# Attention products in two halves of 64 rows, low parts of the exponentials on GpSimd, and four smaller moves

## Chip, core and metric

The kernel runs on one core of one Trainium2 chip. The metric is the device time of one launch over all 8 images, in microseconds (us). Before the change it is 9249.9 us, the median of 3 runs (9244.49 to 9249.97).

## What is computed

The reference has two layers on x of shape (8, 192, 64, 64). The first (`_L0_conv_ref`) is a layer norm over channels, a projection, a 3x3 depthwise convolution, a selective scan in four directions, a norm, a gate and an output projection. The second is attention over all 4096 positions of an image, with 96 channels:

```python
theta_x = _conv1x1(x, theta_w, theta_b).reshape(B, O, N)   # O = 96, N = 4096
phi_x = _conv1x1(x, phi_w, phi_b).reshape(B, O, N)
g_x = _conv1x1(x, g_w, g_b).reshape(B, O, N)
f1 = jnp.einsum('bon,bom->bnm', theta_x, phi_x)
f_div_C = jax.nn.softmax(f1, axis=-1)
y = jnp.einsum('bnm,bom->bon', f_div_C, g_x)
W_y = _conv1x1(y.reshape(B, O, H, W), W_w, W_b)
return W_y + x
```

All of the change lies in the second layer and in the step that makes its operands.

## The kernel before

Each image runs through a projection stage, a scan stage, a mix stage (`run_mix`: it finishes layer 0 chunk by chunk and makes phi, g and the first theta) and an attention stage (`run_attend`). A chunk is 512 positions (T); there are 8 chunks (NCH). Engines run in order and meet at semaphores only; the order of the work is written out by hand.

**Precision.** An operand of the attention's products is a pair of 4-byte values rounded to fp32r: the high part is the value rounded, the low part is the rest. Scores are phi high times theta high, plus phi low times theta high, plus phi high times theta low; the weighing is g high times p high, plus g low times p high, plus g high times p low, where p is the exponential. `phh`, `phl` hold phi (97 rows by 4096), `thc[par]` holds theta of a chunk twice (high and low, 97 rows by 512), `gth`, `gtl` hold g with a column of ones for the denominator.

**The shift.** The exponentials need the top score of each query subtracted. Row 96 of `phh` is 1 and row 96 of `thc[par][0]` holds minus the top, so that the scores' product adds it. For the next chunk the tops come from 32 products per chunk, high times high (`top`, L601, 96 rows), which VectorE reduces (L1384); `TOPS` (L287) says how many of them go into each step: none in step 0, 2 in steps 1 to 4, 3 in steps 5 to 12, none in 13 to 15. VectorE then reduces the 32 tops to one (`negate`, L1395) and SP writes the row with 4 DMAs (L382), which it issues behind the two stores of the chunk before (`store`, L361).

**A step.** A chunk has 16 steps (mp). Step mp on TensorE, in `attend` (L736): `scores` (L675, 6 products of 97 rows for two blocks of 128 keys, into two PSUM banks), then up to two tops, then `weigh` of step mp-2 (L698, 6 products of 128 rows, all adding into bank 4), then a third top if there is one. The other engines: ScalarE takes the exponential out of PSUM (L1014, `pf`) and rounds it (L1020, `ph`; waits until `weigh` of mp-2 has read the old one); VectorE subtracts (L1400, `pl`), after the step's tops; TensorE weighs it two steps later. In step 0 TensorE makes theta of the next chunk (L598, L599, with fp32 operands), which ScalarE copies twice (L962, L965) and VectorE subtracts (L1315, one instruction). At step 2 ScalarE reads the sum of the chunk before (L1002, `yraw`); its denominator goes to DRAM and back (`invert`, `divide`), and the output products (L732, 96 rows by 128 and by 64 columns, fp32) stand at the ends of steps 10 and 12. The last chunk has no tops and no theta; the first has nothing of a chunk before.

```python
for e in range(2):                       # scores, L687 on
    mm(dst, kk, hi[:, :], ...)           # L692
    q = mm(dst, phl[...], hi[:, :], ...) # L693
    q = mm(dst, kk, lo[:, :], ...)       # L695
```

GpSimd does nothing in the attention stage.

Of the kernel before, what the change touches and what calls it, by code (L numbers as in the profile page):

```python
# [19 lines left out]
F32 = mybir.dt.float32  # L20
# [34 lines left out]
def build(nc, nb, x, vec, w_in, w_x, w_dt, sel, fold, ident, w_out, w_att, gb, w_w, out):  # L55
# [3 lines left out]
    with ctx:  # L59
# [23 lines left out]
        rdb = sb("rdb", [O, T], where=aty)  # L83
# [7 lines left out]
        phh = sb("phh", [O + 1, L], F32R, where=kx)  # L91
        phl = sb("phl", [O + 1, L], F32R, where=kx)
# [46 lines left out]
        thc = [[sb(f"thc{q}{i}", [O + 1, T], F32R, where=vx) for i in range(2)] for q in range(2)]  # L139
# [13 lines left out]
        oa = sb("oa", [P, T], where=lnx)  # L153
        phf = sb("phf", [O, T], where=lnx)
        zs = sb("zs", [P, 2, T], where=lnx)
        cs = sb("cs", [P, 2, T], where=lnx)
        tapw = sb("tapw", [P, 6, P], where=lnx)
# [29 lines left out]
        def barrier(eng, b, n):  # L187
# [8 lines left out]
            "pads_set", "rows_zero", "row_one", "xb_zero", "bias_row", "consts_set", "dsum_set", "borders_set", "scan_set", "att_set", "thc_set", "mx_link",  # L196
# [14 lines left out]
            "thc_ready", "st_ready", "pf_ready", "ph_ready", "pl_ready", "pv_ready", "yraw_ready", "den_ready", "inv_link", "rden_ready",  # L211
# [75 lines left out]
        TOPS = [0] + [2] * 4 + [3] * 8 + [0] * 3  # L287
# [3 lines left out]
        DEN_AT, RB_AT, WY_AT, WR_AT = 5, 8, 10, 12  # L291
# [3 lines left out]
        def _(sp):  # L295
# [15 lines left out]
            with sp.Fori(0, nb) as b:  # L311
# [55 lines left out]
                def attend(c, par, before, nxt):  # L367
# [3 lines left out]
                    if before:  # L371
# [5 lines left out]
                        sp.dma_start(rdb[:, :], rden.unsqueeze(0).to_broadcast([O, T])).then_inc(S["rb_loaded"], 16)  # L377
                        store(c - 1)
                    if nxt:
                        sp.wait_ge(S["nmx_ready"], i + 2)  # L380
                        for t in range(4):
                            sp.dma_start(thc[1 - par][0][O:O + 1, t * P:(t + 1) * P].bitcast(F32), nmr[:, t:t + 1].bitcast(F32))\  # L382
                                .then_inc(S["shift_loaded"], 16)
# [8 lines left out]
        def _(pe):  # L392
# [24 lines left out]
            with pe.Fori(0, nb) as b:  # L417
# [183 lines left out]
                def top(j, i, par, t, m, bank):  # L601

                    if j == 0:
                        pe.wait_ge(S["thh_ready"], i + 1)
                    pe.wait_ge(S["top_read"], i * NU + (j + 1))
                    mm(ps[:, bank, :], thc[par][0][0:O, t * P:(t + 1) * P], phh[0:O, bass.ds(m * T, T)],  # L606
                       start=True, stop=True).then_inc(S["top_ready"], 1)

                def early_top(c, t):
# [6 lines left out]
                    mm(ps[:, 6 + t % 2, :], thc[0][0][0:O, t * P:(t + 1) * P], phh[0:O, bass.ds(m * T, T)],  # L616
# [58 lines left out]
                def scores(mp, c, i, par, first):  # L675
                    s = i * MP + mp
                    hi, lo = thc[par]
                    early = mp == 0 and first
                    if mp == 0 and not first:
                        pe.wait_ge(S["thl_ready"], i + 1)  # L680
                        pe.wait_ge(S["shift_loaded"], b * (64 * (NCH - 1)) + (c * 64 + 64))
                    pe.wait_ge(S["pf_ready"], s + 1)
                    if early:
                        for e in range(2):
                            mm(ps[:, e, :], phh[:, e * P:(e + 1) * P], lo[:, :], start=True, stop=False)
                        shift(i)
                        pe.wait_ge(S["thc_ready"], b + 1)  # L687
                    for e in range(2):
                        m = 2 * mp + e
                        dst = ps[:, 2 * (mp % 2) + e, :]  # L690
                        kk = phh[:, m * P:(m + 1) * P]
                        mm(dst, kk, hi[:, :], start=not early, stop=False)  # L692
                        q = mm(dst, phl[:, m * P:(m + 1) * P], hi[:, :], start=False, stop=early)  # L693
                        if not early:
                            q = mm(dst, kk, lo[:, :], start=False, stop=True)  # L695
                    q.then_inc(S["st_ready"], 1)

                def weigh(mp, i):  # L698
                    s = i * MP + mp
                    pe.wait_ge(S["pl_ready"], s + 3)  # L700
                    if mp == 0:
                        pe.wait_ge(S["yraw_ready"], i + 1)
                    for e in range(2):
                        m = 2 * mp + e
                        dst = ps[0:O + 1, 4, :]
                        mm(dst, gth[:, m, :], ph[:, mp % 2, e, :], start=(m == 0), stop=False)  # L706
                        mm(dst, gtl[:, m, :], ph[:, mp % 2, e, :], start=False, stop=False)  # L707
                        q = mm(dst, gth[:, m, :], pl[:, mp % 2, e, :], start=False, stop=(m == MT - 1))  # L708
                    q.then_inc(S["pv_ready"], 1)
# [26 lines left out]
                def attend(c, par, before, nxt):  # L736
                    i = i_0 + c
                    for mp in range(MP):
                        scores(mp, c, i, par, not before)
                        if mp == 0 and nxt:  # L740
                            theta(c + 1, i + 1, before)
                        blocks = range(FIRST_TOP[mp], FIRST_TOP[mp] + TOPS[mp]) if nxt else ()
                        for j in blocks[:2]:
                            top(j, i + 1, 1 - par, j // (NU // 4), j % (NU // 4), 5 + j % 2)
# [783 lines left out]
```

## Time and profile before

| what | value |
|---|---|
| median of 3 runs | 9249.9 us |
| profiled execution | 9256.15 us |
| its span | 9254.4 us |
| instructions | 103902 |
| PE busy | 8642.6 us, 93% |
| PE weight loads | 4648.4 us, 50% |
| DVE busy | 7377.0 us, 80% |
| ACT busy | 6091.9 us, 66% |
| POOL busy | 3295.4 us, 36% |

PE is TensorE, PEld its weight loads (they run beside the products), DVE VectorE, ACT ScalarE, POOL GpSimd, SP the engine that issues the DMAs. A product's time in the trace runs from its start to its last result, and products overlap, so that PE's busy share says little; the distance between the starts of two products is its pace. Lines (L692) are those of the kernel before.

### The profile page before, as it was taken

To read this page: it belongs to the slowest core of one execution; us is meant where nothing else is said; L and a number is where in the kernel's file an instruction comes from. 1 tells how busy PE (TensorE), PEld (TensorE's weight loads), DVE (VectorE), ACT (ScalarE), POOL (GpSimd) and SP (SyncE) were. 2 spreads that over 40 slices of the span, in tenths; PEclk is the share of its full clock that TensorE was granted. 3 is DMA by queue.
4 is the path that set the end of the run, shared out by engine and by line. 5 is a ranking of instruction groups with operands and counts; after the bars stand their busy time and mean duration, and the time that the engine had idled before them with its cause. 6 is when DMAs were issued, how large, how long until landed. Compare 5 with 4: busy or idle time off the path is not lost. (4 is left out here: it accounts for less than half of the span.)

```text
span 9254.4 us, 103902 instructions
## 1 busy us (share of the span) xinstructions
PE 8642.6 (93%) x26448; PEld 4648.4 (50%) x26448; DVE 7377.0 (80%) x8229; ACT 6091.9 (66%) x7440; POOL 3295.4 (36%) x1853
## 2 busy tenths in 40 slices
PE   7899998999989998899988999889998899988999
PEld 3336743367433674336733367333673336733476
DVE  6987779877798777987679876798767987689876
ACT  6765677656776567765677556775567755677566
POOL 2870028600286002860038600385003850038400
PEclk9999999999999999999999999999999999999999
DMA  1320013200132001320013200232002320023200
GB/s 53 111 87 13 10 56 112 80 13 10 57 111 82 11 11 59 115 76 10 11 63 111 76 10 11 65 116 71 8 12 68 111 73 8 11 72 114 66 8 12
DMA packets 286693, 503.21 MB, mean 54 GB/s; under 512 B 142155, under 2 KB 143215, under 8 KB 253431
## 3 DMA queue, kind: packets, MB, share of 16 engines
q1 hardware_dynamic: 286199, 497.81, 17.9%
q8 instruction: 166, 2.72, 0.1%
q14 instruction: 328, 2.69, 0.1%
HBM read 467.99 MB, written 29.47 MB: 54 GB/s over the span
## 5 line engine op out<-in xcount | busy, mean ns | idle before, releaser
L1400 DVE TENSOR_TENSOR pl<-pf,ph 128x1024 fp32r<-128x1024 f32 x1024 | 1254.3, 1225 | 1007.1 <-ACT ph L1020 999.5
L1253 DVE TENSOR_TENSOR_SCAN h<-ps,h,dbu 128x512 f32<-128x512 f32 x1536 | 1884.2, 1267 | 59.8 <-POOL dbu L1087 29.9
L1087 POOL TENSOR_TENSOR dbu<-bs,du 128x1024 f32<-128x1024 f32 x768 | 1808.1, 2369 | 54.1 <-POOL du L1078 54.1
L1020 ACT ACTIVATE ph<-pf 128x1024 fp32r<-128x1024 f32 x1024 | 1085.3, 1060 | 750.3 <-PE ps L708 750.0
L885 ACT ACTIVATE ps<-dt,negA 128x512 f32<-128x512 f32 x1536 | 1037.5, 687 | 684.8 <-DVE h L1253 684.8
L1014 ACT ACTIVATE pf<-ps 128x1024 f32<-128x1024 f32 x1024 | 1050.4, 1026 | 530.7 <-PE ps L695 513.3
L1066 POOL MEMSET pad<- 128x66 f32 (+1 forms) x64 | 7.2, 200 | 3853.2 <-DVE fa L1429 3853.0
L1384 DVE TENSOR_REDUCE mx<-ps 128x1 f32<-128x512 f32 x1792 | 1168.6, 683 | 78.8 <-PE ps L606 62.5
L1261 DVE TENSOR_TENSOR hc<-h,ps 128x1024 f32<-128x1024 f32 x768 | 937.9, 1221 | 110.3 <-PE ps L487 19.7
L487 PE MATMUL ps<-xhl,selr 128*128 128x512 f32 x1536 | 768.1, 585 | 238.8 <-DVE hc L1261 238.6
L1072 POOL TENSOR_TENSOR dt<-dt,ze 128x1024 f32<-128x1024 f32 x256 | 604.0, 2359 | 1061.3 <-ACT dt L878 1061.3
L692 PE MATMUL ps<-thc,phh 97*128 97x512 f32 x2048 | 847.2, 414 | 6.1 <-ACT thc L997 6.1
L1078 POOL TENSOR_TENSOR du<-dt,u 128x512 f32<-128x512 f32 x512 | 712.1, 1411 | 317.1 <-DVE dt L1243 316.4
L706 PE MATMUL ps<-ph,gth 128*97 128x512 f32 x2048 | 818.9, 400 | 3.2 <-ACT yraw L1002 3.2
L693 PE MATMUL ps<-thc,phl 97*128 97x512 f32 x2048 | 815.6, 398 | 0.0
L708 PE MATMUL ps<-pl,gth 128*97 128x512 f32 x2048 | 808.2, 395 | 0.0
L707 PE MATMUL ps<-ph,gtl 128*97 128x512 f32 x2048 | 807.8, 394 | 0.0
L695 PE MATMUL ps<-thc,phh 97*128 97x512 f32 x2032 | 802.2, 395 | 0.0
L487 PEld LDWEIGHTS ps<-xhl,selr 128*128 128x128 f32 x1536 | 248.1, 193 | 896.7 <-DVE hc L1261 716.5
L606 PE MATMUL ps<-phh,thc 96*128 96x512 f32 x1792 | 614.6, 403 | 18.6 <-DVE mx L1384 17.9
L528 PE MATMUL ps<-hc,eye 128*128 128x512 f32 x1024 | 484.0, 595 | 0.0
L692 PEld LDWEIGHTS ps<-thc,phh 97*128 97x128 f32 x2048 | 389.7, 190 | 171.9 <-issue 66.7
(204 smaller groups left out, 14540.6 us busy)
## 6 DMA issues: line engine op xcount, KB each, us to landing
bs<-rows SPq DMA_DIRECT2D x256, 1024.0 KB, 5.1
bs<-rows SPq DMA_DIRECT2D x512, 256.0 KB, 6.1
xa<-in_x SPq DMA_DIRECT2D x130, 256.0 KB, 2.9
xb<-in_x SPq DMA_DIRECT2D x130, 128.0 KB, 3.0
out<-fa SPq DMA_DIRECT2D x64, 256.0 KB, 2.1
rdb<-rden SPq DMA_DIRECT2D x56, 192.0 KB, 3.4
out<-fa SPq DMA_DIRECT2D x64, 128.0 KB, 2.4
xhl<-ct SPq DMA_DIRECT2D x256, 8.0 KB
```

Source lines behind the costliest of these rows:

```text
L487: m = mm(flat(ps[:, 4 + e, :]), selr[:, j * P:(j + 1) * P], src, start=True, stop=True)
L692: mm(dst, kk, hi[:, :], start=not early, stop=False)
L693: q = mm(dst, phl[:, m * P:(m + 1) * P], hi[:, :], start=False, stop=early)
L706: mm(dst, gth[:, m, :], ph[:, mp % 2, e, :], start=(m == 0), stop=False)
L885: A(ps[:, 2 + e, :], dt[par][:, 0 if j < NS else 1, :], ACT.Exp, scale=negA[:, k * NT + j:k * NT + j + 1]).then_inc(S["dA_ready"], 1)
L1014: A(pf[:, mp % 2, :, :], ps[:, 2 * (mp % 2):2 * (mp % 2) + 2, :], ACT.Exp)\
L1020: A(ph[:, mp % 2, :, :], pf[:, mp % 2, :, :], ACT.Copy).then_inc(S["ph_ready"], 1)
L1087: pool.tensor_tensor(dbu[:, q, :, :], bs[par][:, q, :, :], du[:, r:r + 1, :].to_broadcast([P, 2, T]), ALU.mult).then_inc(S["dbu_ready"], 1)
L1253: dve.tensor_tensor_scan(h[:, j, ::step], ps[:, 2 + e, ::step], dbu[:, q, e, ::step], h[:, j, end:end + 1], ALU.mult, ALU.add)\
L1261: TT(hc[:, q, :, :], h[:, 2 * q:2 * q + 2, :], ps[:, 4:6, :], ALU.mult).then_inc(S["hc_ready"], 1)
L1384: dve.tensor_reduce(mx[:, t, m:m + 1], ps[:, 5 + j % 2, :], AX.X, ALU.max)\
L1400: TT(pl[:, mp % 2, :, :], pf[:, mp % 2, :, :], ph[:, mp % 2, :, :].bitcast(F32), ALU.subtract)\
```

## The change

- **Halves of 64 rows.** phi's three tensors become `ph1` (rows 0 to 95 high, 96 to 127 high of rows 64 to 95 again), `ph2` (rows 0 to 95 low, 96 to 127 high of rows 32 to 63) and `ph3` (33 rows at partition 0 for even blocks, 33 rows at 64 for odd ones, the last of each being 1 for the shift). Theta is laid out to match in `th1`, `thx` and `thy`. Scores of a block are now five products of 64 rows or fewer, and those of two blocks are ten: six in `scores_1`, four in `scores_2`. Even products run over partitions 0 to 63 into one bank, odd ones over 64 to 127 into the other; `scores_2` turns the banks round. `weigh` becomes twelve halves, the lower rows into bank 4 and the upper into bank 5, and is split in two calls of six. A top becomes two halves into the same bank, the second waiting until the first is complete (`top_half`).
- **Order on TensorE.** A step is `scores_1` (with a third top around it), half of `weigh` (with a top), `scores_2`, the other half of `weigh` (with a top).
- **GpSimd** subtracts `pl` in the steps that have tops; VectorE in the others, one step later in its order, ahead of the tops.
- **TOPS** is now 0, 0, 2, then 3 in steps 3 to 12, 0 in 13 to 15. The output products move to the ends of steps 13 and 15.
- **The sums** of banks 4 and 5 are read by ScalarE and VectorE and added on VectorE; ScalarE reads ahead of its rounding in step 1.
- **The shift's row** is written by two DMAs of 512 elements (into `thx` and `thy`) ahead of the chunk's stores.
- ScalarE copies theta a third time (`thx`), and phi four times more in the mix stage; VectorE subtracts theta in four instructions instead of one (steps 1, 4, 5, 6).

```diff
-        TOPS = [0] + [2] * 4 + [3] * 8 + [0] * 3
+        TOPS = [0] * 2 + [2] + [3] * 10 + [0] * 3
-        DEN_AT, RB_AT, WY_AT, WR_AT = 5, 8, 10, 12
+        DEN_AT, RB_AT, WY_AT, WR_AT = 5, 8, 13, 15
+        LOW, UP = slice(0, R), slice(R, P)
+        BY_POOL = [mp for mp in range(MP) if TOPS[mp]]
...
@@ sync, attend
-                        sp.dma_start(rdb[:, :], rden...).then_inc(S["rb_loaded"], 16)
-                        store(c - 1)
+                        sp.dma_start(rdb[0:O, :], rden...).then_inc(S["rb_loaded"], 16)
                     if nxt:
                         sp.wait_ge(S["nmx_ready"], i + 2)
-                        for t in range(4):
-                            sp.dma_start(thc[1 - par][0][O:O + 1, t * P:(t + 1) * P]..., nmr[:, t:t + 1]...)
+                        for row in (thx[1 - par][LO:LO + 1, :], thy[1 - par][O:O + 1, :]):
+                            sp.dma_start(row..., nmr[:, :]...).then_inc(S["shift_loaded"], 16)
+                    if before:
+                        store(c - 1)
@@ tensor
+                def top(j, i, c, par, rows):
+                    n = b * (NU * (NCH - 1)) + c * NU + (j + 1)
+                    t, m = j // (NU // 4), j % (NU // 4)
+                    if rows == LOW:
+                        if j == 0:
+                            pe.wait_ge(S["thh_ready"], i + 1)
+                            pe.wait_ge(S["thl_ready"], i * 4 + 1)
+                        pe.wait_ge(S["top_read"], i * NU + (j + 1))
+                    else:
+                        pe.wait_ge(S["top_half"], n)
+                    q = mm(ps[:, 6 + j % 2, :], th1[par][rows, :]..., ph1[rows, m * T:(m + 1) * T],
+                           start=(rows == LOW), stop=(rows == UP))
+                    q.then_inc(S["top_half" if rows == LOW else "top_ready"], 1)
+                def scores_1(mp, c, i, par, first, j=None):
...
+                    def low(n):
+                        if n < 2:
+                            return mm(ps[:, bank, :], (ph1, ph2)[n][LOW, one], t1[LOW, :], start=(n == 0), stop=False)
+                        return scores_0(mp, par, 0)
+                    def up(n):
+                        if n < 2:
+                            return mm(ps[:, bank + 1, :], (ph1, ph2)[n][UP, other], (t1, tx)[n][UP, :], start=(n == 0), stop=False)
+                        return scores_0(mp, par, 1)
+                    if j is not None:
+                        top(j, i + 1, c, 1 - par, LOW)
+                    for n in range(2 if mp == 0 and first else 3):
...
+                    q.then_inc(S["s1_done"], 1)
+                    if j is not None:
+                        top(j, i + 1, c, 1 - par, UP)
+                def scores_2(mp, i, par, first):
+                    pe.wait_ge(S["s1_done"], i * MP + (mp + 1))
...
+                    mm(ps[:, bank, :], ph1[UP, one], t1[UP, :], start=False, stop=False)
+                    mm(ps[:, bank + 1, :], ph1[LOW, other], t1[LOW, :], start=False, stop=False)
+                    mm(ps[:, bank, :], ph2[UP, one], tx[UP, :], start=False, stop=not early)
+                    q = mm(ps[:, bank + 1, :], ph2[LOW, other], t1[LOW, :], start=False, stop=not early)
...
+                def weigh(mp, e, i, c, par=0, j=None):
...
+                    for n in range(3):
+                        if j is not None and n == 1 - e:
+                            top(j, i + 1, c, 1 - par, LOW)
+                        if j is None or n < 1 - e:
+                            half(n, 4, LOW)
+                            q = half(n, 5, UP)
+                        else:
+                            half(n, 5, UP)
+                            q = half(n, 4, LOW)
...
+                    if j is not None:
+                        top(j, i + 1, c, 1 - par, UP)
@@ scalar
+                    A(thx[par][R:O, :], thf[R:O, :], ACT.Copy).then_inc(S["thx_ready"], 1)
...
+                        A(ph1[O:P, bass.ds(c * T, T)], phf[R:O, :], ACT.Copy)
+                        A(ph2[O:P, bass.ds(c * T, T)], phf[LO:R, :], ACT.Copy)
+                        for e in range(2):
+                            A(ph3[e * R:e * R + LO, ...], blocks[:, :, e, :], ACT.Copy).then_inc(S["ph3_ready"], 1)
...
-                        if mp == LAG and before:
-                            read_sum(i - 1)
                         act.wait_ge(S["st_ready"], s + 1)
-                        act.wait_ge(S["pl_ready"], s + 1)
+                        wait_low(act, i, mp - 2)
                         A(pf[...], ps[...], ACT.Exp).then_inc(S["pf_ready"], 1)
                         if mp == 0 and nxt:
                             split_theta(i + 1, 1 - par)
+                        if mp == LAG - 1 and before:
+                            read_sum(i - 1)
@@ gpsimd
+                    for mp in BY_POOL:
+                        pool.wait_ge(S["ph_ready"], i * MP + (mp + 1))
+                        pool.tensor_tensor(pl[:, mp % 2, :, :], pf[...], ph[...], ALU.subtract).then_inc(S["plp_ready"], 1)
@@ vector
+                def read_sum(i):
+                    dve.wait_ge(S["pv_ready"], i * MP + (MP + 2))
+                    dve.tensor_copy(rdb[:, :], ps[0:O + 1, 5, :]).then_inc(S["sum5_read"], 1)
+                    dve.wait_ge(S["sum4_read"], i + 2)
+                    dve.wait_ge(S["sum5_read"], i + 2)
+                    TT(yraw[:, :], yraw[:, :], rdb[:, :], ALU.add).then_inc(S["yraw_ready"], 1)
...
-                        if mp == 1 and nxt:
-                            low_theta(i + 1, 1 - par)
+                        if mp in (1, 4, 5, 6) and nxt:
+                            low_theta(i + 1, 1 - par, (1, 4, 5, 6).index(mp))
+                        if mp == LAG and before:
+                            read_sum(i - 1)
...
+                        if mp > 0 and mp - 1 in BY_DVE:
+                            low_exp(mp - 1, i * MP + (mp - 1))
+                        for j in tops[0:]:
+                            top(j, i + 1)
```

## Rows read from the trace of the kernel before

**Rows 1.** Busy time by stretch: the attention stage of the first image.
```profile
core 0: us, PE busy (x) PEld busy (x) DVE busy (x) ACT busy (x) POOL busy (x), PEclk, DMA share, GB/s
741.00:1180.00 439.00, 435.11 (x1776) 311.13 (x1775) 309.45 (x392) 272.16 (x272) 0.00 (x0) 0.99 0.04 9
```

**Rows 2.** Timeline in the attention stage: start us, us, engine, line, operation.
```profile
849.95 0.39 PE L695 MATMUL ps<-thc,phh 97*128 97x512 f32 x1
...
850.65 0.40 PE L695 MATMUL ps<-thc,phh 97*128 97x512 f32 x1
...
851.08 1.02 ACT L1014 ACTIVATE pf<-ps 128x1024 f32<-128x1024 f32 x1 [1.71 <-PE ps L695]
...
852.27 0.39 PE L692 MATMUL ps<-thc,phh 97*128 97x512 f32 x1
```

**Rows 3.** Timeline of ScalarE: theta's first copy in two chunks that follow each other.
```profile
861.31 0.68 ACT L962 ACTIVATE thf<-ps,vecs 96x512 f32<-96x512 f32 x1 [0.86 <-PE ps L599]
...
918.11 0.68 ACT L962 ACTIVATE thf<-ps,vecs 96x512 f32<-96x512 f32 x1 [0.86 <-PE ps L599]
```

**Rows 4.** Timeline of TensorE: the first output product, later theta's two fp32 products.
```profile
840.45 1.03 PE L732 MATMUL ps<-yn,ww 96*128 96x512 f32 x2
840.91 0.79 PE L692 MATMUL ps<-thc,phh 97*128 97x512 f32 x1
841.54 0.39 PE L693 MATMUL ps<-thc,phl 97*128 97x512 f32 x1
...
859.22 1.02 PE L598 MATMUL ps<-pad,wa 128*96 x2
860.17 1.10 PE L599 MATMUL ps<-pad,wa 64*96 x2
861.20 0.47 PE L706 MATMUL ps<-ph,gth 128*97 128x512 f32 x1
861.50 0.39 PE L707 MATMUL ps<-ph,gtl 128*97 128x512 f32 x1
```

**Rows 5.** Timeline in the mix stage: products of only 96 columns, two to a line.
```profile
657.87 0.39 PE L654 MATMUL ps<-wa,na 128*128 128x96 f32 x2
658.09 0.39 PE L655 MATMUL ps<-wa,nb 128*128 128x96 f32 x2
```

**Rows 6.** Costliest groups of the page: busy us, mean ns of one, idle before.
```profile
L1400 DVE TENSOR_TENSOR pl<-pf,ph 128x1024 fp32r<-128x1024 f32 x1024 | 1254.3, 1225 | 1007.1 <-ACT ph L1020 999.5
L1087 POOL TENSOR_TENSOR dbu<-bs,du 128x1024 f32<-128x1024 f32 x768 | 1808.1, 2369 | 54.1 <-POOL du L1078 54.1
L1020 ACT ACTIVATE ph<-pf 128x1024 fp32r<-128x1024 f32 x1024 | 1085.3, 1060 | 750.3 <-PE ps L708 750.0
L1014 ACT ACTIVATE pf<-ps 128x1024 f32<-128x1024 f32 x1024 | 1050.4, 1026 | 530.7 <-PE ps L695 513.3
L1384 DVE TENSOR_REDUCE mx<-ps 128x1 f32<-128x512 f32 x1792 | 1168.6, 683 | 78.8 <-PE ps L606 62.5
```

**Rows 7.** Timeline of ScalarE in steps 0 to 2 of the second chunk.
```profile
804.52 0.68 ACT L962 ACTIVATE thf<-ps,vecs 96x512 f32<-96x512 f32 x1 [0.86 <-PE ps L599]
805.24 0.63 ACT L965 ACTIVATE thc<-thf 96x512 fp32r<-96x512 f32 x1
...
810.33 0.58 ACT L1002 ACTIVATE yraw<-ps 97x512 f32<-97x512 f32 x1
```

**Rows 8.** Timeline in the projection stage: GpSimd beside a VectorE instruction with two SBUF inputs.
```profile
169.22 0.75 DVE L1190 SCALAR_TENSOR_TENSOR u<-pad,vecs,u 128x512 f32<-128x512 f32 x1
...
170.52 2.46 POOL L1072 TENSOR_TENSOR dt<-dt,ze 128x1024 f32<-128x1024 f32 x1 [117.50 <-ACT dt L878]
...
170.79 2.73 DVE L1190 SCALAR_TENSOR_TENSOR u<-pad,vecs,u 128x512 f32<-128x512 f32 x1
```

**Rows 9.** Timeline of ScalarE in a step of the mix stage.
```profile
681.74 0.49 ACT L985 ACTIVATE gth<-ps 128x384 f32 x1 [0.34 <-PE ps L655]
...
686.26 0.63 ACT L791 ACTIVATE sqa<-da 128x512 f32<-128x512 f32 x1 [4.03 <-DVE db L1163]
```

More of the change, by code:

```diff
@@ L138, in build @@
         thf = sb("thf", [O, T], where=vx)
-        thc = [[sb(f"thc{q}{i}", [O + 1, T], F32R, where=vx) for i in range(2)] for q in range(2)]
+        th1 = [sb(f"th1{q}", [P, T], F32R, where=vx) for q in range(2)]
+        thx = [sb(f"thx{q}", [P, T], F32R, where=vx) for q in range(2)]
+        thy = [sb("thy0", [P, T], F32R, where=vx)]
         mx = sb("mx", [P, 4, NU // 4], where=vx)
@@ L673, in shift @@
                     q.then_inc(S["shift_ready"], 1)
-                def scores(mp, c, i, par, first):
+                def scores_1(mp, c, i, par, first, j=None):
                     s = i * MP + mp
-                    hi, lo = thc[par]
+                    if mp == 0 and not first:
+                        pe.wait_ge(S["thl_ready"], i * 4 + 4)
+                        pe.wait_ge(S["thx_ready"], i + 1)
+                        pe.wait_ge(S["shift_loaded"], b * (32 * (NCH - 1)) + (c * 32 + 32))
+                    pe.wait_ge(S["pf_ready"], s + 1)
+                    bank = 2 * (mp % 2)
+                    one, other = slice(2 * mp * P, (2 * mp + 1) * P), slice((2 * mp + 1) * P, (2 * mp + 2) * P)
+                    t1, tx = th1[par], thx[par]
+                    def low(n):
[9 more added lines that the diff above has]
+                    for n in range(2 if mp == 0 and first else 3):
+                        if j is None:
+                            low(n)
+                            q = up(n)
+                        else:
+                            up(n)
+                            q = low(n)
+                    q.then_inc(S["s1_done"], 1)
+                    if j is not None:
+                        top(j, i + 1, c, 1 - par, UP)
@@ new lines, in scores_0 @@
+                def scores_0(mp, par, e, stop=False):
+                    rows = (slice(0, LO + 1), slice(R, O + 1))[e]
+                    return mm(ps[:, 2 * (mp % 2) + e, :], ph3[rows, mp * P:(mp + 1) * P], (thx, thy)[e][par][rows, :], start=False, stop=stop)
+                def scores_2(mp, i, par, first):
+                    pe.wait_ge(S["s1_done"], i * MP + (mp + 1))
+                    bank = 2 * (mp % 2)
+                    one, other = slice(2 * mp * P, (2 * mp + 1) * P), slice((2 * mp + 1) * P, (2 * mp + 2) * P)
+                    t1, tx = th1[par], thx[par]
@@ L767, in _ @@
                 for mp in range(MP - LAG, MP):
-                    weigh(mp, last)
+                    for e in range(2):
+                        weigh(mp, e, last, NCH - 1)
                 turn_den(last)
@@ L1373, in step @@
                         else:
-                            low_theta(i, 0)
+                            for n in range(4):
+                                low_theta(i, 0, n)
                 add_rem(0, 0)
-                for q in range(2):
-                    dve.memset(thc[q][1][O:O + 1, :].bitcast(F32), 0.0).then_inc(S["thc_set"], 1)
                 run_mix(dve, step)
```

163 lines of the change are left out of this document (89 added, 74 removed).

## The prediction

> **What bounds the kernel now.** The change lies in the attention stage, so I read the busy times by stretch first. Of the 439 us from 741 to 1180, PE is busy 435, DVE 309, ACT 272 and POOL 0, at a granted clock of 0.99 [rows 1]. A busy PE may only be a PE with long products in flight, so the timeline comes next: from the product at 849.95 to the one at 852.27 are ten distances, 0.232 us each [rows 2]. Everything that streams 512 columns of fp32r costs TensorE one such slot, whether it has 96, 97 or 128 rows. A chunk has 16 steps of 12 products and 32 tops, 224 slots, 52.0 us. Theta's two products are 0.86 us each and the outputs the same (840.45 to 841.54 is 1.09: 0.86 and one slot [rows 4]), 3.4 us together, and changes to a narrow tile 0.33 at theta (below), taken as the same at the 64-column output: 56.1. The chunk's period is 918.11 - 861.31 = 56.80 us [rows 3]. So TensorE stands still for 0.7 us of 57; its count of slots is the time. ACT and DVE wait for it: 750 us before the rounding for L708, 1007 before `pl` for ACT [rows 6].
>
> **What the change takes away.** Five halves of 64 rows stand for three products of 97, so two blocks cost ten halves where they cost six products. If two halves on different rows run side by side in one slot, scores are 5 slots instead of 6; `weigh` stays at 6 (twelve halves), a top at 1 (two). 16 slots per chunk go: 16 x 0.232 = 3.7 us; over 64 chunks 1024 slots, 238 us. That is the ceiling.
>
> **Does a pair fit a slot?** No row shows two halves side by side; rows only bound it. Each half needs a weight load of its own. Where products have only 96 columns, a load and a product follow the last pair after (658.09 - 657.87)/2 = 0.11 us [rows 5]; two are 0.22, under 0.232. The lower bound is no saving in the slot but the pair itself, 0.22; the upper is two slots, no overlap, 0.464. I take 0.232, since loads keep up and each row half has its own columns to stream as before. 64 chunks have 13,056 pairs, so each ns of a pair is worth 13 us: the result hangs on this more than on anything.
>
> **What it adds on TensorE.**
> - Tile shape. Theta's 64-row product costs more than 1.72 for the four fp32 instructions: from 859.22 to 861.50 is 2.28 us, less 1.72 and one slot leaves 0.33 for changing shape and back; the 96*128 output cost none [rows 4]. Now 64 rows is the common shape: theta and the second output change there and back as before, the first output newly does. +0.33 per chunk from the second on.
> - Tops in the first half of `weigh`. The upper half may not be loaded before the lower one is complete: 0.39 (a product's time [rows 2]), some 0.05 to pass the semaphore, and 0.11 for its load = 0.55 us after the lower's start. Its place is two slots behind, 0.46. The next half in order is an upper one again, so the 0.08 is not caught up: 11 steps, +0.9 per chunk. Bounds: 0 and 0.2 each. The other two tops have three slots and wait for nothing, as does `s1_done`, except in the two steps of chunk 0 that have no `weigh`.
> - The start of the new sum (step 2, `weigh` of 0). It needs banks 4 and 5 read and `pl` of 0. Counted from the end of theta: ACT copies 0.68 and 0.63 with 0.1 of gaps [rows 7], then `thx` 0.6, rounds 1.06, takes the next exponential 1.03 [rows 6] and reads the sum 0.58 [rows 7]: 4.7 us. DVE behind the rounding: `pl` 1.23 and the copy of bank 5, 0.69 (a reduction of this size is 0.68 [rows 6]): 5.05; with 0.1 for semaphore and load 5.15. TensorE is there after 3 + 11 + 3 = 17 slots and 0.24 of leaving the narrow tile: 4.2. It waits 0.9 us per chunk; reading the sum ahead of the rounding keeps it from being 1.1 more.
>
> **The low parts on GpSimd.** POOL takes 2.37 us for 128x1024 against DVE's 1.23 [rows 6]. From the start of the last scores' product to ACT is 0.43 (850.65 to 851.08 [rows 2]); then 1.03 + 1.06 + 2.37, and 0.2 of gaps, 0.1 for the load: 5.15 us to the weighing. In steps of three tops (14 slots) it is due 23 slots later, 5.33: hidden, by 0.2. In steps without tops DVE does it: 3.97 against 18 slots, 4.17. In the last chunk steps have 11 slots but POOL still does 11 of them. There two steps less four slots must hold 5.15, so a step is 3.04 us instead of 12 slots, 2.78: 11 x 0.26 = +2.9, the other five steps give 1.2, the tile shape takes 0.3: the last chunk gets 2.0 longer. DVE loses 11 x 1.23 us per chunk, gains 3 x 0.68 for theta and 1.4 for the sums; it is no bound.
>
> DVE and POOL collide where DVE reads two SBUF inputs: the L1190 beside a POOL instruction ran 2.73 us where the one before took 0.75 (it ended 0.5 us after POOL did), and POOL took 2.46 [rows 8] instead of 2.37 [rows 6]. In the attention stage this can hit three `low_theta` and the divide per chunk. `low_theta` comes behind the last top of a step, 0.8 us into the next; POOL ends the old `pl` 0.5 and begins the new 1.5 us into it (a step's end, 0.4, 1.06). They pass each other; 0, up to 1 us each if not.
>
> **The rest.** Theta's four subtractions and ACT's `thx` add to chunk 0 only what is in the 0.9. In the mix stage ACT's four new copies, about 2.2 us, lie in the 4.03 us that it waits behind L985 [rows 9]: nothing; without that cover 14 us per image. The shift's row: two DMAs instead of four, with SP past its stores; it has steps 14 and 15 to land, over 5 us. Nothing either way. POOL's two rows of ones go behind the barrier into 100 free us. Per image: a second row copied at the start 0.6, the last sum's addition 0.75, theta's copies in the first mix step 0 to 1: +1.2.
>
> **Sum per image.** Chunk 0: -3.7 + 0.9 + 0.9 + 0.9 (its two bare steps wait for `s1_done`, and scores' start) = -1.0. Chunks 1 to 6: -3.7 + 0.33 + 0.9 + 0.9 = -1.6 each, -9.6. Chunk 7: +2.0, of which I drop 0.5 since its first steps run ahead. Outside: +1.2. Together -7.9, over 8 images -63 us. The profiled execution was 9256.15 us: 9193. The median stands 6 below it: **9187 us**.
>
> A rule that speaks against this. The profile shows only that loads and products follow each other every 0.11 us [rows 5]. The Trainium skill (TensorE: Matmul & The Clock Gate, Part 3) gives 3.07 times for four 32-row products side by side. By that, four cost 1.3 of one; a pair at 1.3 slots would be 0.30 us and the sum some 900 us the other way. No run here shows it.
>
> **Rivals.**
> - **A: the halves run staggered** (slower). If the second half's load starts only when the first half's product does, it starts 0.11 us behind. Alternating halves cost nothing, but where two of the same rows meet (twice a step: into `scores_2` and out of it) the other half idles for the stagger. 32 per chunk less the 11 already charged, 21 x 64 = 1344 times 0.11 = 148 us, some 25 of it inside waits counted above: 9187 + 123 = 9310. It decides from a stagger of 0.05 us on. For it: no row shows a load going ahead of more than one product. Against it: there every product used all rows, so no load could go ahead. The same section of the Trainium skill says loads are pulled ahead where rows differ, starts 4 ns apart. No row tests it.
> - **B: pairs are quicker**, or the top's half waits for nothing. At 0.22 a pair, a step of three tops is 14 x 0.22 + 0.08 = 3.16 against my 3.33 (POOL's chain would hold it at (5.15 + 5 x 0.22)/2 = 3.13): of the 13 us per ns some 9 are left beside the waits of step 2 and the last chunk, 12 x 9 = 108 us, 9080. Without the top's 0.9 alone, 7 x 8 x 0.9 = 50 us, 9137.
> - **C: a pair takes 0.24 or more**, from loads, or four instructions per slot: +8 x 13 = 107 us, 9290.
> - **D: halves one behind the other**, at the upper bound of 0.464: 13,056 x 0.232 = 3029 us more, 12,200.
> - **E: the change doesn't shorten the stage**, since POOL's 2.37 is 3.0 beside DVE: a step of three tops is (5.78 + 5 x 0.232)/2 = 3.47, and 0.14 x 77 of them = 11 us per image, less 3 that the sum counts as waits: +63 us, 9250.
>
> **Chances.** My case 0.56, B 0.18, A 0.13, C 0.05, D 0.02, E 0.06. Runs differ by little, so about 0.2% (19 us) tells a change. Faster by over that: my case less 0.04 for its edge, and B: 0.70. Within: 0.04 + 0.06 = 0.10. Slower: A, C, D = 0.20. The range from B's 9080 to A's 9310 leaves out D and the ends of B and C.
>
> **What would show it.** Right: a chunk's period (L962's successor) near 55.2; two halves starting within 0.01 us of each other and pairs 0.232 apart; steps of three tops at 3.33; 0.9 us before the first `weigh` of a chunk; steps of 3.0 in the last chunk, PE waiting for POOL there; mix stage as before. Wrong: starts of halves evenly 0.11 apart with a hole at each turn of the banks (A); PE waiting for POOL in every step (E); a `low_theta` of 2 us; a granted clock below 0.98.

## The result, and the profile after

The changed kernel takes 9380.8 us (median; 9371.6 to 9390.2) against 9249.9 us: ratio 1.014, 95% interval 1.0125 to 1.016. It is slower, by 131 us, where 9187 was forecast with 9080 to 9310 as range.

The head of the page of the changed kernel, its busy times by engine:

```profile
span 9374.9 us, 133193 instructions
PE 8578.1 (92%) x38480; PEld 4852.5 (52%) x38480; DVE 6843.5 (73%) x7829; ACT 6268.4 (67%) x7768; POOL 4955.9 (53%) x2557
```

TensorE is as busy as before for a work of fewer slots. The costliest groups show why one has to look closer: the tops' loads.

```profile
L1220 POOL TENSOR_TENSOR pl<-pf,ph 128x1024 fp32r<-128x1024 f32 x704 | 1687.1, 2396 | 2771.3 <-ACT ph L1109 2771.3
...
L629 PE MATMUL ps<-ph,th 64*128 64x512 f32 x3584 | 1469.1, 471 | 0.0
...
L629 PEld LDWEIGHTS ps<-ph,th 64*128 64x128 f32 x3584 | 980.3, 306 | 139.6 <-DVE mx L1484 9.4 <-issue 1.3
```

A top's load takes 306 ns; a load of as many rows and columns for the scores (L713) takes 188 in the same trace.

The timeline where scores meet the weighing (it answers to [rows 2]), products of TensorE only:

```profile
916.66 0.39 PE L713 MATMUL ps<-th,ph 64*128 64x512 f32 x1
916.67 0.39 PE L718 MATMUL ps<-thx,ph 64*128 64x512 f32 x1
916.90 0.39 PE L736 MATMUL ps<-thx,ph 33*128 33x512 f32 x1
916.90 0.39 PE L736 MATMUL ps<-thy,ph 33*128 33x512 f32 x1
917.13 0.39 PE L770 MATMUL ps<-ph,gth 64*97 64x512 f32 x2
```

Halves on different rows start 0.00 to 0.01 us apart and the pairs 0.23 apart. The heart of the change works. The copies of theta on ScalarE (answers to [rows 3]), first and last start of the image's eight:

```profile
L1042 ACT ACTIVATE thf<-ps,vecs x8: 682/684/684, 661.5 to 1104.0; 96x512 f32<-96x512 f32 x8
```

Before it is 659.8 to 1088.5. Those between stand at 753.92, 809.95, 867.12, 927.50, 984.72 and 1046.80: behind the first chunk periods of 57.2 us, and two of 60.38 and 62.08, where before has 56.80. The timeline of TensorE between 867.12 and 927.50, where the loop's one pass ends and the next begins:

```profile
918.75 0.39 PE L770 MATMUL ps<-pl,gth 64*97 64x512 f32 x2
919.07 1.07 PE L807 MATMUL ps<-yn,ww 96*64 96x512 f32 x2
921.69 0.49 PE L713 MATMUL ps<-th,ph 64*128 64x512 f32 x1 [1.55 <-issue]
...
923.44 0.63 PE L745 MATMUL ps<-th,ph 64*128 64x512 f32 x1
```

From 919.07 to 921.69 is 2.6 us for an output that took under 1.1 at [rows 4]; "issue" says that TensorE waited for nothing which the profile shows. Products then take 0.63 instead of 0.39, at a granted clock of 0.53, nearly the lower of the two levels (1.2 GHz). By stretches, the first of them short and the others of a chunk, TensorE's busy time, granted clock, DMA share and GB/s:

```profile
923.00:926.50 3.50, 3.50 (x12) 0.53 0.18 40
...
809.00:866.00 57.00, 55.83 (x426) 1.00 0.04 10
866.00:926.00 60.00, 57.27 (x425) 0.97 0.06 13
926.00:984.00 58.00, 56.82 (x428) 1.00 0.05 11
984.00:1046.00 62.00, 58.92 (x427) 0.94 0.04 11
```

Two periods in each image are long, those in which TensorE jumps back for a further pass of its loop over pairs of chunks. In the mean of the eight images they take 60.07 and 59.72 us, 2.9 and 2.5 more than their neighbours; the first image, shown here, has 3.2 and 4.9. TensorE's own wait at the sixteen jumps is 1.40 to 1.95 us.

Where the time went, per image, from ScalarE's first copy of theta (L962, after L1042), means of eight images (the last column of seven):

```
us                     mix to chunk 0  chunk 0  chunks 1 to 5  chunks 6, 7, next start   sum
before                      90.03       55.05      283.97           720.66            1149.71
after                       93.20       56.15      291.37           723.66            1164.38
plain weights               93.10       54.14      281.31           722.13            1150.68
loop written out            92.55       56.01      285.58           724.41            1158.55
theta first                 92.77       56.35      291.39           722.24            1162.75
all three                   93.21       54.66      276.35           721.97            1146.19
  + scores first            92.89       52.94      276.33           720.01            1142.17
  + last low parts DVE      93.86       52.95      276.34           717.09            1140.24
```

After stands 14.7 us an image above before, 8 x 14.7 = 117 of the two spans' 120.5. Half of it lies in chunks 1 to 5, where -8.0 was forecast.

### The profile page after: what moved, and what is told of

Same layout as the page of the kernel before. It is cut to its first block and busy times, and to the rows that moved or that the text cites. A ratio compares the mean times of both kernels' runs of the same rounds, so it can differ in the third digit from the quotient of the medians.

```text
span 9374.9 us, 133193 instructions
## 1 busy us (share of the span) xinstructions
PE 8578.1 (92%) x38480; PEld 4852.5 (52%) x38480; DVE 6843.5 (73%) x7829; ACT 6268.4 (67%) x7768; POOL 4955.9 (53%) x2557
## 5 line engine op out<-in xcount | busy, mean ns | idle before, releaser
L1220 POOL TENSOR_TENSOR pl<-pf,ph 128x1024 fp32r<-128x1024 f32 x704 | 1687.1, 2396 | 2771.3 <-ACT ph L1109 2771.3
L629 PE MATMUL ps<-ph,th 64*128 64x512 f32 x3584 | 1469.1, 471 | 0.0
L770 PE MATMUL ps<-ph,gth 64*97 64x512 f32 x4096 | 1058.3, 406 | 109.5 <-DVE rdb L1506 56.5
L770 PE MATMUL ps<-pl,gth 64*97 64x512 f32 x4096 | 1095.0, 394 | 0.0
L770 PE MATMUL ps<-ph,gtl 64*97 64x512 f32 x4096 | 1093.4, 393 | 0.0
L629 PEld LDWEIGHTS ps<-ph,th 64*128 64x128 f32 x3584 | 980.3, 306 | 139.6 <-DVE mx L1484 9.4
L713 PE MATMUL ps<-th,ph 64*128 64x512 f32 x2048 | 661.0, 403 | 27.3 <-issue 27.3
L1500 DVE TENSOR_TENSOR pl<-pf,ph 128x1024 fp32r<-128x1024 f32 x320 | 390.3, 1220 | 259.4 <-ACT ph L1109 259.4
L770 PEld LDWEIGHTS ps<-pl,gth 64*97 64x97 f32 x4096 | 500.0, 159 | 107.6
L770 PEld LDWEIGHTS ps<-ph,gtl 64*97 64x97 f32 x4096 | 512.6, 163 | 69.7 <-issue 12.9
```

Of the source, the lines that this page charges most:

```text
L629: q = mm(ps[:, 6 + j % 2, :], th1[par][rows, :].rearrange("p (k t) -> p t k", t=4)[:, t, :], ph1[rows, m * T:(m + 1) * T], start=(rows == ...
L770: return mm(ps[0:O + 1, bank, :], g[rows, m, :], p[rows, mp % 2, e, :], start=(m == 0 and n == 0), stop=(m == MT - 1 and n == 2))
L1220: pool.tensor_tensor(pl[:, mp % 2, :, :], pf[:, mp % 2, :, :], ph[:, mp % 2, :, :].bitcast(F32), ALU.subtract)\
```

## The experiments

**Tops' lower half one pair sooner.** The wait of the upper half for the lower was a term of the forecast; here it gets room.

```diff
-                        if j is not None and n == 1 - e:
+                        if j is not None and n == 0:
...
-                        if j is None or n < 1 - e:
+                        if j is None:
```

> The lower half of each top product goes one product pair sooner in half of the places, so that at least one more pair (0.23 us) lies between it and its upper half. Theory W (the upper half waits for the end of the lower one, 0.2 us at each of some 11 tops of 56 chunks): about 120 us less than the changed kernel, near 9260, and the steps with three tops take 3.25 to 3.3 us instead of 3.47. Rival S (the reading of the top's weights with a stride of four is what costs, 306 against 188 ns each): the wait only moves, within 30 us of the changed kernel (9350 to 9390), three-top steps stay at 3.47.

Measured 9443.7, ratio to before 1.021 (1.0193 to 1.0227): slower than the changed kernel by 63 us, which neither theory had. The tops' own waits (L629, times of eight images) went from 9.4 us behind `mx` to this:

```profile
  DVE mx L1484: 127.5, 600
  issue: 112.0, 56
  DVE rdb L1506: 70.0, 48
```

A top that comes sooner comes before VectorE has read the bank of the one two before it, and in the chunk's third step it stands behind the wait for the read of the sum, ahead of the weighing. The steps with three tops take 3.53 us instead of 3.47, where theory W had 3.25 to 3.3. W's gain doesn't appear, but the edit brought waits of its own; the next run decides between the two.

**Plain weights.** The same tops, of queries side by side instead of every fourth.

```diff
-  th1[par][rows, :].rearrange("p (k t) -> p t k", t=4)[:, t, :]
+  th1[par][rows, t * P:(t + 1) * P]
...
-  sp.dma_start(row.bitcast(F32).rearrange("o (p j) -> o p j", j=4), nmr[:, :].bitcast(F32))
+  for t in range(4):
+      sp.dma_start(row[:, t * P:(t + 1) * P].bitcast(F32), nmr[:, t:t + 1].bitcast(F32))
```

> The tops' weights are read without a stride, 128 neighbouring columns; for that each chunk's shift goes out in 8 transfers of 128 elements instead of 2 of 512, and the output is the same. Theory S (the stride costs 0.12 us in each of the two loads of some 11 tops of 56 chunks, 0.24 together): 70 to 140 us less than the changed kernel, 9240 to 9310, and the top's loads take near 190 ns. Theory W (the wait between the halves costs, whatever the stride): no more than 30 us less. The six more transfers at the chunk's end are off the path by either theory.

Measured 9274.9, ratio 1.0022 (1.0012 to 1.0032): 106 us less than the changed kernel. The load's group, of this kernel:

```profile
L630 PEld LDWEIGHTS ps<-ph,th 64*128 64x128 f32 x3584 | 650.5, 185 | 146.6 <-DVE mx L1485 41.6 <-issue 1.3
```

How a load that is 0.12 us longer costs a slot is seen in the changed kernel, at the end of a step with three tops; all loads and products of TensorE between:

```profile
894.29 0.31 PEld L629 LDWEIGHTS ps<-ph,th 64*128 64x128 f32 x1
894.30 0.39 PE L770 MATMUL ps<-pl,gth 64*97 64x512 f32 x1
894.30 0.60 PE L629 MATMUL ps<-ph,th 64*128 64x512 f32 x1
894.30 0.18 PEld L746 LDWEIGHTS ps<-th,ph 64*128 64x128 f32 x1
894.50 0.20 PEld L745 LDWEIGHTS ps<-th,ph 64*128 64x128 f32 x1
894.53 0.39 PE L746 MATMUL ps<-th,ph 64*128 64x512 f32 x1
...
894.75 0.39 PE L745 MATMUL ps<-th,ph 64*128 64x512 f32 x1
```

L745 belongs beside L746, but its load is on the same rows as the top's and starts 0.20 us after L746's; its product goes a slot later, with L746's successor's. One half is then alone in its slot. L746 starts at 894.53 and in the next step at 898.01: 3.48 us, 15 slots for 14 pairs, just what the step had before. With plain weights seven of a chunk's ten such steps take 3.26 to 3.30 us (distances of ScalarE's exponentials, means of chunks 1 to 5), 14 slots, and hold no wait between a top's halves worth a slot. Theory S holds. The other three take 3.50, 3.32 and 3.53: in them VectorE subtracts a part of theta (L1418) ahead of its tops, and TensorE waits for the bank. Of this kernel, VectorE and then a load:

```profile
823.96 0.68 DVE L1418 TENSOR_TENSOR thx<-thf,th 32x512 fp32r<-32x512 f32 x1
824.67 1.29 DVE L1485 TENSOR_REDUCE mx<-ps 128x1 f32<-128x512 f32 x2
...
825.42 0.18 PEld L630 LDWEIGHTS ps<-ph,th 64*128 64x128 f32 x1 [0.34 <-DVE mx L1485]
```

That is 0.5 us a chunk which the forecast had at nothing; no run moved these subtractions.

A sentence of the Trainium skill bears on the load (SBUF — State Buffer, Door 1): memory is read in lines of 16 bytes, and an access that crosses to a new line each time pays. Four fp32 are 16 bytes, so this stride has a new line for every weight; by that rule the edit should speed up the load, and the trace agrees (306 to 185 ns). The same passage names four fp32 as how far one can stride for free; taken so, it does not agree: a stride of four is not free here.

**Loop written out.** TensorE's alone.

```diff
-                run_attend(pe, attend)
+                for c in range(NCH):
+                    attend(c, c % 2, c > 0, c < NCH - 1)
```

> TensorE's loop over the attention's chunks is written out, eight bodies one after the other; nothing else changes. Theory L (where the loop jumps back, twice in an image, TensorE stands 1.6 to 2.4 us without instructions and runs at the lower clock level for some us after; such chunks take 60.4 and 62.1 us against 57.2): -8 us an image, -64 in all, near 9317, and all middle chunks take 57.2. Rival: the holes come from the supply of instructions as such, and are at other places then: within 20 us of the changed kernel.

Measured 9334.2, ratio 1.0089 (1.0072 to 1.0106): -47 us. The theta copies stand at 869.82, 927.00, 984.11, 1041.15 and 1098.20: chunks of 57.04 to 57.18, no long ones. Theory L holds: the holes are gone and none came elsewhere. Its -64 took the first image's two long periods for all eight; chunks 1 to 5 give 5.8 us an image, which is nearly the whole of the 47, and what else moves in the table (-0.65, +0.75) cancels.

**Theta first.**

```diff
+                        if isinstance(c, int) and c == 0:
+                            split_theta(i, 0)
                         A(ph1[O:P, bass.ds(c * T, T)], phf[R:O, :], ACT.Copy)
...
-                        if isinstance(c, int) and c == 0:
-                            split_theta(i, 0)
```

> In the first step of the mix stage ScalarE splits theta ahead of its four copies of phi instead of behind them. Theory M (the low part of theta on VectorE waits 10.1 us for these copies in the first step, and what comes behind it, phi's low parts of the next step, waits with it: the step lasts 19.6 us against 12.6 before): the step comes down by 4 to 7 us, -32 to -56 in all, 9325 to 9350. Rival: the copies of phi are then late instead, and the time stays within 10 us of the changed kernel.

Measured 9364.7, ratio 1.0125 (1.0108 to 1.0142), 16 us below the changed kernel, half of the least that theory M had (32). The intervals of the two overlap, but the table has -1.6 an image too, 13 us. In the first image phi's copy (L1062) comes 19.63 us behind the last one in the changed kernel, 12.55 before, 14.80 here. What made the 19.63 is seen in the timeline of the changed kernel, first of ScalarE:

```profile
660.62 0.85 ACT L1073 ACTIVATE ph<-phf 32x256 fp32r<-32x256 f32 x2
661.49 0.68 ACT L1042 ACTIVATE thf<-ps,vecs 96x512 f32<-96x512 f32 x1
...
667.04 0.63 ACT L871 ACTIVATE sqa<-da 128x512 f32<-128x512 f32 x1 [3.55 <-DVE db L1261]
```

then of TensorE:

```profile
668.24 2.08 PE L417 MATMUL ps<-sqa,avg 128*128 128x512 f32 x2 [4.28 <-ACT sqb L872]
670.11 1.91 PE L418 MATMUL ps<-sqb,avg 128*128 128x512 f32 x2
```

Theta waits 2.3 us behind phi's new copies; the squares come 5.55 behind theta instead of 3.28, since VectorE makes four subtractions (0.7 each) where it made one; and TensorE, after 4.28 us idle, takes 2.08 for two products that take 1.13 in this experiment, where it was idle for 1.98: the granted clock over 665 to 677 us is 0.72 there and 1.00 here. That third part, 2.5 us, and the first are gone in this experiment; the second stays. In the means of the eight images this step lasts 12.55 us before, 19.08 in the changed kernel and 15.39 here: 3.7 less, of which 2.7 are left at the attention's first theta copy and 1.6 in an image. What takes the rest was not found.

**The three together.** The short diffs above at once.

> The changed kernel with three edits at once: the tops' weights without a stride (with 8 transfers for the shift), TensorE's loop over chunks written out, theta split ahead of the copies of phi. Theory T (three separate losses, which one after another measured -106, -47 and -16 against the changed kernel's 9381): they add up to -169, 9212, ratio to before 0.996 (0.9945 to 0.9975), and every middle chunk takes 55.3 us. Rival: the loads and the holes share a cause, the sum is less than the terms, the time stays at 9235 to 9275 and is not below the kernel before.

Measured 9231.8, ratio 0.9983 (0.9974 to 0.9992). A middle chunk takes 55.27 us; the forecast said 55.2. The sum of the three was to give 9212; 20 us are missing, spread over the columns of the table (1.2 us an image up to chunk 0, 0.5 in chunk 0, 0.8 in chunks 1 to 5 where both the stride's and the loop's terms lie, 0.5 behind), so the terms overlap somewhat. The result lies between the two theories' times, nearer to the rival's 9235 to 9275, but unlike it below the kernel before. The interval leaves out no change, but by little: 19 us.

**Control: before with its loop written out.** The edit is that of the third experiment.

> The kernel before with TensorE's loop over chunks written out, nothing else. Theory B (the hole at the jump back comes with the changed kernel's longer body; before has chunk periods of 56.79 us throughout, the jump included): no change, 9240 to 9262. Rival (any jump costs, and before hides or spreads it): -20 to -60.

Measured 9251.3, ratio 1.0000 (0.9991 to 1.0009). Theory B: before had no hole to lose.

**Control: before with strided tops.**

```diff
-  thc[par][0][0:O, t * P:(t + 1) * P]
+  thc[par][0][0:O, :].rearrange("p (k t) -> p t k", t=4)[:, t, :]
...
```

> The kernel before with its 96-row top products' weights read with a stride of four, and the shift sent in one transfer of 512 elements for each chunk, as the change has it; the output is the same. Theory S (a strided load takes 0.306 us, 0.074 more than the 0.232 of a product that could cover it): 32 tops in 56 chunks by 0.074 = +133 us, 9383; at least +80. Rival (it is the split in halves that makes the strided load count, each half's load standing before a pair): within 20 us of before.

Measured 9282.5, ratio 1.0036 (1.0023 to 1.005): +31 us, in between, nearer to the rival. The load is as slow:

```profile
L605 PEld LDWEIGHTS ps<-phh,thc 96*128 96x128 f32 x1792 | 505.2, 310 | 115.8 <-DVE mx L1383 59.3
```

But chunks grow by 0.40 us, 0.013 for a top, where the stride costs 2.0 us, 0.063 for a top, in the changed kernel. In a line of whole products a late load hardly delays the next; in halves it costs its partner's company. My +133 took a slow load as lost time whole, which is wrong in either kernel.

**Scores first in the chunk's third step.** Added to the three together.

```diff
+                        if mp == LAG:
+                            scores_2(mp, i, par, not before)
                         if mp >= LAG:
                             weigh(mp - LAG, 0, i, c, par, blocks[0])
...
-                        scores_2(mp, i, par, not before)
+                        if mp != LAG:
+                            scores_2(mp, i, par, not before)
```

> As the kernel with the three edits undone, and in the chunk's third step the second half of the scores goes ahead of the first product with the values, so that the wait for the new sum of two banks (1.2 us in 48 chunks, 56.5 in all) has two pairs and their own wait, 0.5 to 0.9 us, ahead of it. Theory R (the wait is on the path): -20 to -45 us against that kernel. Rival (the scores' second half waits for the first half's end instead, or VectorE is as late at the next place): within 10 us of it.

Measured 9207.3, ratio 0.9955 (0.9941 to 0.9969), 24 us less than without. But the middle chunks are the same to 0.02 us. The wait for the sum, in the changed kernel

```profile
932.59 0.47 PE L770 MATMUL ps<-ph,gth 64*97 64x512 f32 x2 [1.18 <-DVE rdb L1506]
```

and in this one

```profile
921.03 0.48 PE L771 MATMUL ps<-ph,gth 64*97 64x512 f32 x2 [0.37 <-DVE rdb L1511]
923.47 0.49 PE L630 MATMUL ps<-ph,th 64*128 64x512 f32 x1 [0.26 <-DVE mx L1489]
```

is shorter (of `rdb` 0.37 instead of 1.18), but the weighing starts 5.09 us after theta's copy (915.94) against 5.10 with the three edits alone (922.84 after 917.74), and the next step 9.49 against 9.50: VectorE sets both. The gain is in chunk 0 (-1.7) and behind chunk 6 (-2.0). Both theories hold for a part each.

**The last chunk's low parts on VectorE.** On top of that, and then alone.

```diff
-                    for mp in BY_POOL:
+                    for mp in (BY_POOL if nxt else []):
...
-                        if mp > 0 and mp - 1 in BY_DVE:
+                        if mp > 0 and (mp - 1 in BY_DVE or not nxt):
```

> As the kernel with the three edits undone and the third step's scores first (9207), and in an image's last chunk, where VectorE has no tops, the low parts of the exponentials are made by VectorE instead of GpSimd. Theory G (GpSimd's chain holds the last chunk's steps at 3.11 us on average, where the three engines' own work is 2.6 to 2.8): 12 steps by 0.3 to 0.5 = -4 to -6 an image, -30 to -50, near 9167, and the steps take 2.6 to 2.8 us. Rival (the steps there are held by ScalarE's two passes of 1.0 and 1.06 us or by TensorE's order): within 10 us of 9207.

> The changed kernel with this one edit: VectorE makes the last chunk's low parts. Theory G: -30 to -50 against 9381, near 9340. Rival: within 10 us of 9381.

Measured 9183.3, ratio 0.9927 (0.9913 to 0.994), and alone 9342.3, ratio 1.0098 (1.0082 to 1.0113): -24 and -39 us. Alone it is in the range of theory G (-30 to -50), on top of the others it falls short of it. The timeline of the last chunk of the changed kernel, TensorE at every second step:

```profile
1188.04 0.48 PE L770 MATMUL ps<-ph,gth 64*97 64x512 f32 x2 [0.71 <-POOL pl L1220]
1194.20 0.47 PE L770 MATMUL ps<-ph,gth 64*97 64x512 f32 x2 [0.72 <-POOL pl L1220]
```

and ScalarE's exponentials, one for each step:

```profile
1189.56 1.03 ACT L1101 ACTIVATE pf<-ps 128x1024 f32<-128x1024 f32 x1 [1.40 <-PE ps L748]
1192.22 1.03 ACT L1101 ACTIVATE pf<-ps 128x1024 f32<-128x1024 f32 x1 [0.53 <-PE ps L748]
1195.72 1.03 ACT L1101 ACTIVATE pf<-ps 128x1024 f32<-128x1024 f32 x1 [1.39 <-PE ps L748]
```

Two steps last 6.16 us, 3.08 each (forecast 3.04). With VectorE, and the other edits, the exponentials of the last chunk come every 2.56 us, eleven slots, TensorE's own count:

```profile
1157.00 1.03 ACT L1106 ACTIVATE pf<-ps 128x1024 f32<-128x1024 f32 x1 [0.44 <-PE ps L749]
1159.57 1.03 ACT L1106 ACTIVATE pf<-ps 128x1024 f32<-128x1024 f32 x1 [0.45 <-PE ps L749]
```

The version with all five edits is 0.7% faster than the kernel before and 198 us faster than the changed one.

**Before with a longer body.** Is it the length of the loop's body that makes the hole?

```diff
+                def padding():
+                    for _ in range(2):
+                        pe.sem_inc(mark, 1)
...
+                        padding()
                         q = mm(dst, phl[:, m * P:(m + 1) * P], hi[:, :], start=False, stop=early)
```

> The kernel before, its loop kept, with two increments of an unused semaphore put ahead of each of TensorE's score, weighing and top products: 896 instructions more in the loop's body, about as many as the changed kernel's body has more than before's. Theory F (a jump back costs when the body's start is no longer at hand, so the length of the body decides): holes of 1.5 to 2.5 us at the two jumps in each image, those chunks 3 us or more longer than their neighbours, the neighbours at 56.8: +30 to +65 us, 9280 to 9315. Rival: no hole at the jumps; either nothing changes, or, if issuing the increments itself holds TensorE, all chunks grow alike.

Measured 10498.5, ratio 1.134 (1.1325 to 1.1363): the increments hold TensorE (products 0.30 us apart where there are no tops), so the price of the hole can't be read from the sum; that part went as the rival had it. The holes themselves are there, at the two jumps, with periods of 75.74, 82.31, 75.97 and 81.78 us. TensorE waits 3.9 to 5.3 us at the sixteen jumps, where theory F had 1.5 to 2.5. One of them:

```profile
976.91 0.76 PE L698 MATMUL ps<-thc,phh 97*128 97x512 f32 x1 [4.25 <-issue]
```

The page's row of a queue that brings instructions agrees (packets, MB, share of 16 engines). Before:

```profile
q8 instruction: 166, 2.72, 0.1%
```

the changed kernel:

```profile
q8 instruction: 366, 6.00, 0.3%
```

and before with the longer body:

```profile
q8 instruction: 382, 6.26, 0.2%
```

The two kernels with TensorE's loop written out say more. Before, written out:

```profile
q8 instruction: 231, 3.78, 0.2%
```

and the changed kernel, written out:

```profile
q8 instruction: 342, 5.60, 0.3%
```

With its loop the kernel before brings in 65 packets fewer than written out, so its further passes are not brought in again. The changed kernel brings in 24 more than written out: its loop saves nothing.

As the trace counts them, a chunk has 232 products before and 424 after (12 x 16 + 32 + 8 and 22 x 16 + 64 + 8, the fp32 ones of theta and the output being two instructions each), so the body of two chunks has 464 and 848, each with its load: 928 and 1696 instructions, and 1824 with the increments. Waits come on top. A body of 928 jumps back at no cost, 1696 and 1824 do not. Why the hole of the last is more than twice the other's is not shown. The Trainium skill (Runtime: NRT & Kernel Launch, Instruction fetch mechanics) says that a taken branch to a target out of the present window of instructions must wait for a fetch; the traces agree for the changed kernel, with waits of 1.40 to 1.95 us. It puts that window at two pages of 256 instructions; by that the body of 928 would stall too, and the trace of before has no hole. It gives TensorE room for 2048 instructions; these bodies are under that, and at which length the hole appears was not tried.

## Why the prediction was wrong

The forecast had -7.9 us an image, the result is +14.7.

- **Does a pair fit a slot**: right. Pairs stand 0.232 apart, halves start within 0.01 us. Rivals A, C and D fall, and so does the 0.30 us a pair that the forecast set against itself. The step that I held for the one all hangs on was sound.
- **"Loads keep up"**: the step that failed most. It took every load as that of a score. The changed kernel's code reads the tops' weights with a stride of four; their load is 306 ns, and that takes the company of one half in each step with three tops. 3.33 us were forecast for it, 3.48 measured, 3.27 with plain weights. The removal gives 106 us back, 13.7 an image.
- **The tops' half wait**, +0.9 a chunk: near nothing with plain weights (3.27 is 14 slots of 0.232 and 0.02). Rival B had named that. In three steps of a chunk a wait for VectorE's subtractions of theta stands instead, 0.5 us together.
- **No term for the loop.** I did not ask what TensorE does between its passes, where before shows no hole; the change adds 384 products and as many loads to a body of 464. Two holes an image, 2.9 and 2.5 us in the mean with the clock's loss: 47 us of the total.
- **The start of the new sum**: 0.9 forecast, 1.18 measured, right in kind. But it is VectorE's place in the chunk, not an extra: with the wait shortened by 0.8 the chunk stays the same.
- **The mix stage "nothing", theta's copies 0 to 1**: to the first theta of the attention +4.5 us in the first image (749.45 to 753.92); from the copy of phi ahead of the first theta to it, the mean is 93.8 before and 99.2 after. The cover at [rows 9] holds in all steps but the first, where theta's copies stand behind phi's and VectorE's four subtractions behind them; the wait then also let TensorE's clock fall. Of it 16 us of the total come back with theta ahead, the four subtractions remain.
- **GpSimd**: hidden in steps of three tops, as said; in the last chunk 3.08 us a step against 3.04. The terms given for that chain add up to 5.19, not 5.15, which would have made it 3.06. That known loss could be had back for the edit of one condition. Rival E falls: it had 3.47 for a step of three tops, and 3.48 came, but for another reason: `pl` on GpSimd takes 2.40 us, not 3.0, and with plain weights the same steps take 3.27. Nor did a subtraction of theta on VectorE run long beside it: all took 0.7.
- **The sum**: with the two unseen terms and theta's place undone, chunk 0 is -0.4 (forecast -1.0), chunks 1 to 5 are -7.6 (-8.0). That the chunks come so near is partly luck: the 0.9 for the tops' halves is not there, and 0.5 for VectorE's subtractions and 0.3 more at the new sum stand in its place. The rest is +4.5 where +1.1 was forecast (-1.6, +1.5, +1.2): the mix stage's part of it, +3.2, is the term that was also mis-sized. So even with these three undone the kernel is 45 us above the forecast (9231.8 against 9187), 27 of them in this rest.

What stays open: 20 us between the sum of the three edits and their joint run; what the four subtractions cost in the mix stage and in the steps, which no run took back; the body's length from which the hole appears.

## What to carry to other kernels

When products are cut in parts that run side by side, look at each load's access pattern: a late load that a single line of products absorbs leaves a partner alone in its slot, and the step is as long as before. Count the loop's body before and after; where it grows (here from 928 to 1696 loads and products), look for a hole at the jump back, and try the loop written out. A cover found in the steady step (here ScalarE's 4 us) has to be looked for again in the first step, where other work stands in the same queue.

## What the runs showed of the hardware that was not expected

- A strided load of 128 fp32 columns takes 306 to 310 ns against 185 to 189, with 64 rows or with 96; its cost on the path, for each top, is 0.063 us in a stream of halves, 0.013 in a stream of whole products.
- The jump back in TensorE's loop costs 1.55 us of plain idleness in the first instance (1.40 to 1.95 in all sixteen), and as much again by the end of the chunk's period, with products at the lower clock behind it (0.63 us each until the clock is back). With a body of 928 loads and products it costs nothing.
- Two halves with their two loads pass in 0.232 us, but one product with its load and two increments takes 0.30: increments are not free on TensorE's queue.
